# TensorE's program for the experts stage: a loop over sixteen passes with register waits, or all 184 passes written out with constant waits

## What is computed

```python
logits = x @ router_w + router_b
top_w, sel = jax.lax.top_k(logits, TOP_K)          # two of eight experts
top_w = jax.nn.softmax(top_w, axis=-1)
...
gu = x @ Wgu + bgu                                 # 128 -> 512
gate, up = jnp.split(gu, 2, axis=-1)
act = (up + 1.0) * quick_gelu(gate)                # 256
out = act @ Wd + bd                                # 256 -> 128
return (acc + out * w_e[:, None], None)
```

## Time and profile before

| | us |
|---|---|
| median of the runs | 1207.85 |
| profiled execution, its own time | 1216.59 |
| its span | 1214.8 |
| PE busy, share of the span | 1034.6, 85% |
| DVE busy | 891.0, 73% |
| ACT busy | 714.4, 59% |
| POOL busy | 583.1, 48% |

### The profile page before, as it was taken

How to read it: one execution, slowest core, us unless ns; L and a number is a source line. 1 busy time by engine, 2 the same in 40 slices (tenths; PEclk the granted TensorE clock), 3 DMA queues, 4 the chain that set the end, 5 groups by cost and what they waited for, 6 DMA issues and landing times. The chain is left out here.

```text
span 1214.8 us, 39840 instructions
## 1 busy us (share of the span) xinstructions
PE 1034.6 (85%) x12967; PEld 857.2 (71%) x12968; DVE 891.0 (73%) x2181; ACT 714.4 (59%) x1446; POOL 583.1 (48%) x630
## 2 busy tenths in 40 slices
PE   5799999999986887888887840699999999999995
PEld 4477877787763456666666740588888898888984
DVE  5687777777773347877877762488888888888985
ACT  1277665666643257676676620567676767676763
POOL 0425746374676215555655552144444444444443
PEclk9899999999997778999999965799999999999998
DMA  8011101011103001111211219221112111221110
GB/s 308 26 38 28 38 21 35 21 37 29 29 3 105 18 18 41 59 58 59 68 51 60 65 56 142 55 57 50 52 55 56 51 52 48 56 56 52 35 23 1
DMA packets 72324, 64.18 MB, mean 53 GB/s; under 512 B 9812, under 2 KB 58227, under 8 KB 72237
## 3 DMA queue, kind: packets, MB, share of 16 engines
q1 hardware_dynamic: 57132, 43.46, 13.3%
q0 software_dynamic: 10016, 17.16, 4.6%
q10 hardware_dynamic: 5090, 2.32, 1.5%
HBM read 33.44 MB, written 24.72 MB: 48 GB/s over the span
## 5 line engine op out<-in xcount | busy, mean ns | idle before, releaser
L1318 POOL DMA_INDIRECT out<-e_y,e_xg x184 | 183.7, 998 | 77.8 <-issue 77.6
L1366 PE MATMUL e_ps<-e_xt,w_hl 128*128 128x256 f16 x736 | 202.2, 275 | 14.2 <-issue 12.8
L1367 PE MATMUL e_ps<-e_xt,w_hl 128*128 128x256 f16 x736 | 201.8, 274 | 0.0
L1368 PE MATMUL e_ps<-e_xt,w_hl 128*128 128x256 f16 x736 | 201.7, 274 | 0.0
L810 POOL DMA_INDIRECT rows<-m_rows,m_place x128 | 127.5, 996 | 44.4 <-issue 44.4
L251 POOL TENSOR_SCALAR vm<-v,early 128x512 f32<-128x512 f32 x96 | 148.5, 1562 | 0.0
L1383 PE MATMUL e_ps<-w_hl,e_hid_hl 128*128 x736 | 145.6, 220 | 0.0
L1384 PE MATMUL e_ps<-w_hl,e_hid_hl 128*128 x736 | 144.9, 219 | 0.0
L1382 PE MATMUL e_ps<-w_hl,e_hid_hl 128*128 x736 | 144.1, 220 | 0.0
L1443 DVE SCALAR_TENSOR_TENSOR e_hid_hl<-e_hid,e_hid_hl 128x512 f16<-128x512 f32 x184 | 127.4, 692 | 20.0 <-ACT e_hid_hl L1416 19.7
L1437 DVE SCALAR_TENSOR_TENSOR e_hid<-e_ps,e_act 128x512 f32<-128x512 f32 x184 | 125.9, 684 | 15.2 <-ACT e_act L1422 10.9
(11 more groups left out here) (249 smaller groups left out, 2603.6 us busy)
## 6 DMA issues: line engine op xcount, KB each, us to landing
e_xg<-rows SPq DMA_DIRECT2D x92, 133.0 KB
resid<-in_x SPq DMA_DIRECT2D x8, 1024.0 KB, 13.9
xb<-in_x SPq DMA_DIRECT2D x32, 256.0 KB, 2.7
m_rows<-resid SPq DMA_DIRECT2D x32, 256.0 KB, 2.7
out<-e_y,e_xg POOLq DMA_INDIRECT x184, 2.3
m_w_f<-in_L_ffn_gate_up_proj SPq DMA_DIRECT2D x1, 2048.0 KB, 8.2
rows<-m_rows,m_place POOLq DMA_INDIRECT x128, 2.4
rows<-nobody SPq DMA_DIRECT2D x15, 133.0 KB, 10.0
```

What stands on the lines that cost most here:

```text
L1318: nc.gpsimd.indirect_dma_start(out_rows, bass.IndirectOffsetOnAxis(ap=who, axis=0), y[:, slot, i, :], None, bounds_check=B * TOK - 1, oob_ ...
L1366: t.matmul(o, hi, x2[0], start=True, stop=False)
L1367: t.matmul(o, hi, x2[1], start=False, stop=False)
L1368: last = t.matmul(o, lo, x2[0], start=False, stop=True)
```

## The change

In the experts stage TensorE no longer uses `in_turns`. Its program is written out for positions 0 to 187, with the same steps in the same order; slot, block and pass numbers are Python integers, so that all waits are for constants. ScalarE, VectorE, GpSimd and SyncE keep their loops.

```diff
-            in_turns(pe, (1, xT), (2, inner), (4, outer), look=look_up)
+            for p in range(2 * BLOCKS + 4):
+                if p % TURN == 0:
+                    look_up(p // TURN)
+                for lag, f in ((1, xT), (2, inner), (4, outer)):
+                    k = p - lag
+                    if 0 <= k < 2 * BLOCKS:
+                        f(k, k // 2, k % TURN, k // 2 % SLOTS, k // (2 * SLOTS))
```

## The result

The changed kernel takes 1188.3 us (median of 4 runs, 1187.7 to 1191.69), the kernel before 1207.09 us beside it. The ratio is 0.985 (95% interval 0.9826 to 0.9875): 18.8 us less, where 19.4 were forecast. The profiled execution has a span of 1185.9 us and took 1187.7 us itself.

A forecast was written before the change was run, and what follows sets the result against it. TensorE's sequencer was taken to bound the experts stage: 37.25 - 2.4 (steps) - 0.6 (branch, index) + 1.2 (code), taken as 35.5 us a trip, saves 19.4 us with 1 us taken back: 1188.5 us, range 1183 to 1200.

The forecast's parts named there:

- A trip is the sum of the sequencer's steps: Each trip of TensorE's loop (sixteen passes) lasts as long as its sequencer's steps, 37.25 us, against 35.28 us of matmuls.
- Register sums and waits, -2.4 us: In each sixteen passes of TensorE, 28 sequencer steps go and 4 are added, some 0.1 us each: -2.4 us.
- The branch, 0.48 us: At the loop's end the pause is 0.80 us with the branch, 0.32 without: the branch is worth 0.48 us.
- Code, +1.2 us: Written-out passes are new code to fetch, at the price of the loop's first trip: +1.2 us in sixteen passes.
- The sum, 35.45 us against the array's 35.28, taken as 35.5: Sequencer's time for sixteen written-out passes, 37.25 - 2.4 - 0.6 + 1.2 us, beside the matmuls' time; almost equal.
- The lead at the look-up: At turn starts the sequencer must be ahead by more than the look-up takes; 1 us of gain taken back.
- The difference of 8.7 us carried whole: The profiled execution lay 8.7 us above the runs' median, no row says where; kept unchanged in the forecast.
- recording bound: If all 8.7 us were loop steps slowed by being recorded, only 14.1 us can be won: 1193.8 us.
- Only the branch: Rival: register sums lie beside matmuls anyway, only branch and index steps count, 6.1 us: 1202 us; chance 0.07.
- Late code: Rival: some 40 more code blocks each come 1.3 us late, so the kernel is slower: 1227.5 us; chance 0.07.
- The array's floor: Rival: fetching code costs the array nothing, 35.28 us a trip, gain 22.8 us: 1185 us; chance 0.12.
- The pauses stay: Rival: the `x_low` wait holds the lead down, or the sequencer gains less unrecorded: 1194 to 1195.5 us; chance 0.18.

The follow-up runs named there:

- extra_loop: The kernel before with one more already-met wait step in each of TensorE's passes: 1230.47 us, ratio 1.015.
- lean_loop: The kernel before, loop kept, without TensorE waits that other waits already imply (24 of 36 a trip, and 2 register sums): 1198.19 us, ratio 0.9863.
- long_loop: TensorE's turns 1 to 22 as a loop of two trips, eleven turns written out in each body, register sums and waits as in the kernel before: 1224.74 us.
- extra_out: The changed kernel with one more already-met wait step in each of TensorE's passes: 1214.23 us, ratio 1.002 to the kernel before.
- words_early: The changed kernel with all 24 look-up words loaded into registers at the end of TensorE's token mixer program: 1191.52 us, ratio 0.9815 to the kernel before.
- words_ahead: The changed kernel with all 24 look-up words loaded into registers just ahead of the first pass: 1201.37 us, ratio 0.9902 to the kernel before.

## Why the prediction was right

- **A trip is the sum of the sequencer's steps**: shown for the kernel before. Waits that wait for nothing cost 0.107 us each (`extra_loop`), and taking 24 of them away wins 17.1 us with the loop in place (`lean_loop`), where the array's pace ends the gain. One reading behind it was too wide: line 1366 is the only row of TensorE in the stage with idle time that nothing explains, but GpSimd has such a row too (line 1318, 77.6 us of "issue"). That one still has 78.0 us after the change, so it was not what bound the kernel.
- **Register sums and waits, -2.4 us**: 24 steps at 0.1 us. All steps at the 0.107 of a wait would make 2.6; with the sums at 0.09 to 0.10, by their starts, it is 2.2 to 2.4.
- **The branch, 0.48 us**: no run takes it away alone. The last trip of the kernel before, which does not branch back, comes near it. Its second turn, from the chain of the earlier trace rows, ends at 1194.96:

```profile
1158.10 0.28 PE e_ps L1366
...
1176.50 0.28 PE e_ps L1366
```

That is 18.46 us in place of 18.86, 0.40 less; some of it is the two steps that the written-out code behind the loop does not need, while the sum and the untaken branch are still there. With a lead in hand the turn that ends in the branch is 0.2 us longer than the other (`lean_loop`), so the 0.48 us is what the pause is worth only where the sequencer is the bound, as it was.
- **Code, +1.2 us**: some 1.4 and 1.5 us where the sequencer is the bound (`long_loop`, `extra_out`; both are differences that use the forecast's prices for the other steps), nothing where it isn't (`words_early`). The changed kernel lies between.
- **The sum, 35.45 us against the array's 35.28, taken as 35.5**: 35.62 measured, and the array's pace is 35.25 (two turns of `words_early`). With the prices from the runs the sequencer's total is 37.28 less 2.2 to 2.4, less 0.6, plus 1.2 to 1.5: 35.5 to 36.0. That is too coarse to say by how much the sequencer is the slower of the two; that it has no slack, `extra_out` shows. The loop's gain, forecast as 19.4 us with 1 us taken back for the lead, is 19.1. That the two agree to 0.3 us is partly luck: a spread of 0.5 us a trip is some 5 us in eleven.
- **The lead at the look-up**: it does run low there, and holes of 0.05 to 0.07 us are left; without the look-up they are gone (`words_early`). The 1 us taken back stood for something real, though its size was a guess.
- **The difference of 8.7 us carried whole**: right in the outcome, though no row stood behind it. The profiled spans differ by 28.9 us: 19.1 in the loop, 1.2 in turn 0, and 8.5 ahead of the first transpose of the stage (767.3 before, 758.7 after), in code that the change doesn't touch. Of these 8.5 us, 5.1 are in one wait, TensorE's for the stage's first rows, before and then after:

```profile
PE e_ps L1351 <- ACT e_xn L1400: 33.5, 1, 33.5
...
PE e_ps L1351 <- ACT e_xn L1406: 28.4, 1, 28.4
```

The changed kernel itself has 33.2 and 34.0 us there in its two later profiles. In its three profiles the loop differs by under 0.2 us, while the first transpose stands at 758.7, 766.7 and 769.4 and the spans are 1185.9, 1194.4 and 1196.9. So what differs between these executions lies nearly all ahead of the stage; the forecast's recording bound (1193.8 us) would have put it into the loop's steps. Why the earlier part differs so stays open.

The rivals. **Only the branch** falls by `extra_loop` and `lean_loop`. **Late code** falls: no pause of PE in the 22 turns (391.85 of 391.85 us busy), with 108 packets. **The array's floor** was right about free fetching only for a sequencer with slack. The Trainium skill, "Runtime: NRT & Kernel Launch", section "Instruction fetch mechanics", calls the crossing of a block mostly hidden: `words_early` agrees with it (17.63 us a turn with 108 packets), `long_loop` doesn't (1.4 us in sixteen passes). **The pauses stay** by the `x_low` hand-over: the timeline of the changed kernel, to set beside the earlier trace rows, has

```profile
843.29 0.39 PE L1351 MATMUL e_ps<-early,e_xn 128*128 128x128 f32 x2
...
844.36 0.42 DVE L1457 TENSOR_TENSOR e_xt<-e_ps,e_xt 128x256 f16<-128x256 f32 x1 [0.18 <-ACT e_xt L1415]
...
845.60 0.27 PE L1366 MATMUL e_ps<-e_xt,w_hl 128*128 128x256 f16 x1
```

so `x_low` ends at 844.78, 0.82 us ahead of the matmul that needs it, as before the change. So the bound that the forecast put on the lead stands, and it did not keep the lead from covering a look-up nearly whole. In the changed kernel 12 of the loop's 440 waits last longer than 51 ns, 0.6 us more in all: the sequencer does now wait for others at times, far too little to decide.

Of what the forecast said would be seen: turns of 17.7 to 17.8 us (17.74 to 17.91), no sum of line 110 and no row of line 1254, some 104 packets (108), PE at 99% (100%), VectorE at 92% (91.6%). "Some 2 us" of pauses are none by the waits, since what is left is delay between overlapping matmuls.

## What to carry to other kernels

When an engine pauses for nothing that the profile names and its waits all last their minimum, add up its sequencer's steps and set the sum beside the array's time: what the sequencer has too much must go, be it waits (`lean_loop`) or sums and the branch (the change). Below the array's time, look for steps that stand together, as the look-up's do here. Before a loop is written out, look for waits that others imply (24 of 36 here, for 17.1 of the 19.1 us) and for loads that can stand earlier, under cover; writing out costs fetched code, and paid here only because it removed more than it added. Once the sequencer is ahead of the array everywhere, fetched code and waits of 0.4 us cost nothing.

## What was not expected of the hardware

- The price of fetched code isn't a property of the code: some 1.4 to 1.5 us for sixteen passes in `long_loop` and `extra_out`, nothing in `words_early`, with about as many packets.
- A branch back costs 0.22 us where the loop's body stays with the engine, and 3.35 us where it doesn't, with a pause of 4.2 us (`long_loop`). One branch of an earlier stage pays it already, before (3.40 us) and after the change; the row of the changed kernel:

```profile
L136 PEldq COMPARE_BRANCH  x8: 83/218/3408, 214.3 to 693.6; - x8
```

- That a taken branch out of the fetched window must wait for its code is what the Trainium skill says too ("Runtime: NRT & Kernel Launch", "Instruction fetch mechanics"); the 3.35 us above agree.
- Word loads cost 0.67 us each with their steps, when they stand in a row (`words_ahead`; 0.73 in `words_early`), though the load itself lasts 0.30 us.
